# In the second attention, VectorE's product of the query with its rotation table is moved in front of the probabilities' share

## The chip, the cores and the metric

The kernel runs on one core of a Trainium2 chip. The metric is the device time of one execution in microseconds, the median of the runs shown. Five engines work side by side, each through its own in-order list of instructions: TensorE (PE in the profile; its weight loads PEld), VectorE (DVE), ScalarE (ACT), GpSimd (POOL) and SyncE (SP, here the issuer of transfers). They order each other by semaphores: an instruction waits until a counter has reached a value, and those behind it on the same engine wait with it.

## What is computed

Two transformer blocks over 16 batches of 128 rows of 256 values, float32. Each block is an attention against a second input and then a feed-forward part with ternary weights. The change lies in the second attention:

```python
q = rms_norm(x_norm @ Wq.T)                 # 16 heads of 128, batch of 128 rows
k = rms_norm(concat(ctx, x_norm) @ Wk.T)    # 4 key heads, 256 keys
v = concat(ctx, x_norm) @ Wv.T
q, k = rope(q), rope(k)                     # x * cos + rotate_half(x) * sin
probs = softmax(q @ k.T / sqrt(128))        # 4 query heads share a key head
x = x + (probs @ v) @ Wo.T
```

## The kernel before, in words

Five stages follow one another: preparation of the weights, first attention, first feed-forward part, second attention (`part_c`), second feed-forward part. The last four are written as generators that an outer loop advances by one step each, so that neighbouring stages overlap by some steps. In a step, every engine but TensorE takes the earlier stage's instructions first.

`part_c` works on 64 units: 16 batches by 4 groups, a group being one key head with its four query heads. It is a software pipeline with an order written out by hand: in step s each phase treats the unit s minus its lag. The lags are PROJ 4, QK_TURN 5, SCORE 6, PROBS 7, LOWS 8, ATTEND 9, OUT 10. Units 0 to 63 therefore pass PROJ in steps 4 to 67 and PROBS in steps 7 to 70; steps 7 to 67 have both. Every value that goes to TensorE is split into two float16 halves, high and low, and each product is made of three passes.

What a unit needs, with the lines of the profile:

- PROJ: TensorE makes q (six matmuls of 512 columns, L1406), then, once VectorE has let the bank of k and v go (`v_lo`), k and v (L1417). VectorE multiplies q by the table of cosines and sines (`q_cs`, L1330). ScalarE takes the sums of squares of q (L1266, waits for `q_cs`) and k (L1272), evicts v's high half (L1276) and takes the logarithm (L1280) and the reciprocal root `r` (L1301). VectorE scales and rotates k (`k_cs`, L1366, waits for `r`) and makes v's low half (`v_lo`, L1370). GpSimd adds the rotated halves of q (L1189) and splits them (L1193, L1220), and does the same for k (L1223, L1226, L1228); L1202 makes the tables of a later batch.
- SCORE: TensorE makes the scores (L1431); VectorE takes the row maximum (L1351) and turns it into `bias` (L1355); ScalarE takes four exponentials with their row sums in `total` (L1235), the first of them in front of `r`.
- PROBS, one step later: VectorE makes the share, `part` = `total` / 1024 (L1321) and then `share` = 1 / `part` (L1324); ScalarE makes the high halves of the probabilities (`p_hi`, L1252, waits for `share`) in four instructions; VectorE makes the low halves in two pairs, `lows(u, 0)` and `lows(u, 1)` (L1311).
- ATTEND and OUT: TensorE multiplies probabilities by values (L1444) and the result by Wo (L1459); ScalarE and VectorE split the result in between (`a_hi` L1245, `a_lo` L1338).

SP turns the halves by transposing transfers (L1138, L1153, L1159).

In a step of `part_c` VectorE's order is: `part`, `share`, `q_cs`, `a_lo`, `lows` 0, (once per batch the residual, L1345), maximum, `bias`, `lows` 1, `k_cs`, `v_lo`, and then, in one step of four each, the statistics of a new batch (L1376, L1380) or the normalized rows (L1385). The steps with statistics are s = 0, 4, 8, ..., those with rows s = 1, 5, 9, ... ScalarE's order is: `a_hi`, four `p_hi`, the squares of q and k, v's high half, logarithm, (in the steps with rows L1286 and L1289), first exponential, `r`, three exponentials.

Of the kernel before, what the change touches and what calls it, by code (L numbers as in the profile page):

```python
# [21 lines left out]
ALU = mybir.AluOpType  # L22
# [15 lines left out]
def wait(eng, sem, value):  # L38

    if value > 0:  # L40
        eng.wait_ge(sem, value)
# [1012 lines left out]
def part_c(core):  # L1054
# [14 lines left out]
    P_SCALE = 1024.0  # L1069
# [25 lines left out]
    total = c.local("total_c", [P, 2, SHARE])  # L1095
    part = c.local("part_c", [P, 2, SHARE])
    share = c.local("share_c", [P, 2, SHARE])
# [18 lines left out]
    S = {n: c.sem("c_" + n) for n in (  # L1116
        "eps", "stats", "rstd", "y", "y_hi", "y_lo", "tables", "q", "kv", "ss_k", "ss_q", "r", "q_cs", "q_rot", "k_cs",
        "k_rot", "v_hi", "v_lo", "q_hi", "q_lo", "k_hi", "k_lo", "scores", "top", "bias", "exps", "share", "p_hi",
        "p_lo", "attn", "a_hi", "a_lo", "o", "out")}
# [5 lines left out]
    def unit(s, lag):  # L1125

        u = s - lag
        return u if 0 <= u < TOTAL else None

    def batch(s, lag):  # L1130


        u = s - lag
        return u // GROUPS if 0 <= u < TOTAL and u % GROUPS == 0 else None
# [172 lines left out]
    def vector(eng):  # L1307
        def lows(u, half):
            eng.wait_ge(S["p_hi"], 2 * u + half + 1)
            for h in range(2 * half, 2 * half + 2):  # L1310
                last = eng.scalar_tensor_tensor(p_hl[:, u % 2, 1, h, :], s_banks(u)[:, h, :],  # L1311
                                                share[:, u % 2, h:h + 1], p_hl[:, u % 2, 0, h, :],
                                                ALU.mult, ALU.subtract)
            last.then_inc(S["p_lo"], 1)

        for s in range(STEPS + 1):
            probs, proj, score, attend = unit(s, PROBS), unit(s, PROJ), unit(s, SCORE), unit(s, OUT)
            if probs is not None:
                u = probs
                eng.wait_ge(S["exps"], u + 1)  # L1320
                eng.tensor_scalar(part[:, u % 2, :], total[:, u % 2, :], 1.0 / P_SCALE, None, ALU.mult)\  # L1321
                   .then_inc(S["share"], 1)
                eng.wait_ge(S["share"], 2 * u + 1)
                eng.reciprocal(share[:, u % 2, :], part[:, u % 2, :]).then_inc(S["share"], 1)  # L1324
            if proj is not None:
                u, b = proj, proj // GROUPS
                eng.wait_ge(S["tables"], b + 1)
                eng.wait_ge(S["q"], u + 1)
                wait(eng, S["q_rot"], u)
                eng.tensor_tensor(  # L1330
                    q_cs[:, :, :, :],
                    Q_BANK.rearrange("p (h d) -> p h d", h=SHARE).unsqueeze(1).broadcast_to([P, 2, SHARE, HEAD_DIM]),
                    turn["q"][:, b % 2, :, :].unsqueeze(2).broadcast_to([P, 2, SHARE, HEAD_DIM]), ALU.mult)\
                   .then_inc(S["q_cs"], 1)
            if attend is not None:
                u = attend
                eng.wait_ge(S["a_hi"], u + 1)
                eng.scalar_tensor_tensor(a_t[:, u % 2, 1, :], A_BANK, A_SCALE, a_t[:, u % 2, 0, :], ALU.mult,  # L1338
                                         ALU.subtract).then_inc(S["a_lo"], 1)
            if probs is not None:  # L1340
                lows(probs, 0)
            b = batch(s, LAST)
            if b is not None:
                eng.wait_ge(S["o"], GROUPS * (b + 1))
                eng.scalar_tensor_tensor(c.x_rows[:, b, :], O_BANK, 1.0 / (W_SCALE * W_SCALE * P_SCALE * A_SCALE),  # L1345
                                         c.x_rows[:, b, :], ALU.mult, ALU.add).then_inc(S["out"], 1)
            if score is not None:
                u = score
                eng.wait_ge(S["scores"], u + 1)
                wait(eng, S["bias"], u - 1)  # L1350
                eng.tensor_reduce(top[:, u % 2, :], s_banks(u), AX.X, ALU.max).then_inc(S["top"], 1)  # L1351
                eng.wait_ge(S["top"], u + 1)
                eng.wait_ge(S["r"], 2 * (u + 1))
                wait(eng, S["exps"], u - 1)
                eng.scalar_tensor_tensor(bias[:, u % 2, :], top[:, u % 2, :], -1.0, r_q(u), ALU.mult, ALU.mult)\  # L1355
                   .then_inc(S["bias"], 1)
            if probs is not None:
                lows(probs, 1)
            if proj is not None:

                u, b = proj, proj // GROUPS
                eng.wait_ge(S["r"], 2 * (u + 1))
                eng.wait_ge(S["v_hi"], u + 1)
                wait(eng, S["k_rot"], u)
                for n in range(2):
                    last = eng.scalar_tensor_tensor(  # L1366
                        k_cs[:, :, n, :], kv_view[:, n, 0, :].unsqueeze(1).broadcast_to([P, 2, HEAD_DIM]), r_k(u, n),
                        turn["k"][:, b % 2, :, n, :], ALU.mult, ALU.mult)
                last.then_inc(S["k_cs"], 1)
                eng.tensor_tensor(v[:, u % V_SLOTS, 1, :, :], kv_view[:, :, 1, :], v[:, u % V_SLOTS, 0, :, :], ALU.subtract)\  # L1370
                   .then_inc(S["v_lo"], 1)
            b = batch(s, 0)
            if b is not None:
                eng.wait_ge(ffn["out"], b + 1)
                wait(eng, S["stats"], 2 * b)
                eng.bn_stats(stats[:, :], c.x_rows[:, b, :]).then_inc(S["stats"], 1)  # L1376
                eng.wait_ge(S["stats"], 2 * b + 1)
                wait(eng, S["y"], b)
                wait(eng, S["rstd"], 2 * b)
                eng.bn_aggr(mv[:, :], stats[:, :]).then_inc(S["stats"], 1)  # L1380
            b = batch(s, ROWS)
            if b is not None:
                eng.wait_ge(S["rstd"], 2 * (b + 1))
                wait(eng, S["y_lo"], b)
                eng.tensor_scalar(y[:, :], c.x_rows[:, b, :], mv[:, 0:1], rstd[:, :], ALU.subtract, ALU.mult)\  # L1385
                   .then_inc(S["y"], 1)
            yield
# [4 lines left out]
    def tensor(eng):  # L1392
        for s in range(STEPS):
# [69 lines left out]
            yield  # L1463

    return sync, pool, scalar, vector, tensor


# [87 lines left out]
```

## Time and profile before

| | us |
|---|---|
| median of the runs | 799.06 |
| lowest | 797.79 |
| the profiled execution, its own time | 800.01 |
| its span, first to last instruction | 798.3 |
| from the first exponential of step 6 to that of step 66 of `part_c` | 410.28 |

The profiled execution lies 0.1% above the median, and 1.7 us of it lie outside the span. Of the span, 410 us are 60 steps of the second attention. In the rows below, a line of a timeline holds start, duration, engine, line of the kernel, operation, output and inputs, and in brackets the idle time of the engine in front of the instruction with what ended it. Neighbouring instructions of an engine can overlap by some hundredths of a microsecond, so distances are taken from start to start.

### The profile page before, as it was taken

How to read it: one execution, taken by the hardware profiler on the slowest of the kernel's cores; microseconds unless marked ns; L12 is line 12 of the kernel's file. 1: busy time of each engine (PE TensorE's matmuls, PEld its weight loads, DVE VectorE, ACT ScalarE, POOL GpSimd, SP SyncE). 2: the span in 40 equal slices, each digit the busy share in tenths (PEclk: the TensorE clock that was granted, in tenths of full speed). 3: DMA queues.
4: the chain of work that ended last, by engine and by line, in shares of the span. 5: the costliest groups of instructions: out<-in, count | busy, mean ns of one | idle time of the engine just before them, and what ended most of it. 6: DMA issues, size and time to landing. Idle time of an engine off the chain costs nothing. (4 is left out here: it accounts for less than half of the span.)

```text
span 798.3 us, 17290 instructions
## 1 busy us (share of the span) xinstructions
PE 677.3 (85%) x5139; PEld 423.0 (53%) x5139; DVE 661.1 (83%) x1576; ACT 624.3 (78%) x2122; POOL 534.5 (67%) x764
## 2 busy tenths in 40 slices
PE   0075799999578678999999999999999999978995
PEld 0043255455234345666666666666666666645552
DVE  6756556764689769999999999999999999978994
ACT  0556477777399769999999999999999999968661
POOL 1413756663357888888788878887887888753673
PEclk9997599999799989999999999999999999999997
DMA  8502555542024356897887798788879787865244
GB/s 278 199 1 54 138 155 148 142 129 86 11 67 106 64 106 126 147 144 129 148 139 142 127 154 139 134 138 154 139 135 144 143 136 133 153 113 93 58 125 122
DMA packets 323795, 99.80 MB, mean 125 GB/s; under 512 B 294868, under 2 KB 322934, under 8 KB 323446
## 3 DMA queue, kind: packets, MB, share of 16 engines
q1 hardware_dynamic: 323702, 98.70, 61.7%
q8 instruction: 41, 0.67, 0.4%
q14 instruction: 52, 0.43, 0.2%
HBM read 20.01 MB, written 6.29 MB: 33 GB/s over the span
## 5 line engine op out<-in xcount | busy, mean ns | idle before, releaser
L1235 ACT ACTIVATE psum<-psum,arena 128x256 f32<-128x256 f32 x256 | 135.9, 531 | 21.1 <-DVE arena L1355 21.0
L1311 DVE SCALAR_TENSOR_TENSOR arena<-psum,arena 128x256 f16<-128x256 f32 x256 | 110.9, 474 | 1.1 <-ACT arena L1252 1.1
L1252 ACT ACTIVATE arena<-psum,arena 128x256 f16<-128x256 f32 x256 | 100.3, 474 | 7.4 <-issue 3.4
L1444 PE MATMUL psum<-arena 128*128 128x512 f16 x384 | 94.2, 381 | 8.1 <-DVE arena L1338 7.9
L1189 POOL TENSOR_TENSOR arena<-arena 128x512 f32<-128x512 f32 x64 | 81.1, 1267 | 27.8 <-DVE arena L1330 27.8
L1406 PE MATMUL psum<-wq_t,arena 128*128 128x512 f16 x384 | 94.5, 383 | 5.5 <-ACT arena L1266 2.8
L1431 PE MATMUL psum<-arena 128*128 128x256 f16 x768 | 95.6, 275 | 1.0 <-DMA arena<-arena 0.8
L1459 PE MATMUL psum<-wo_t,arena 128*128 128x256 f16 x768 | 95.0, 274 | 0.1
L305 ACT ACTIVATE arena<-psum 128x1024 f32<-128x1024 f32 x64 | 63.1, 1019 | 33.2 <-PE psum L391 33.2
L1459 PEld LDWEIGHTS psum<-wo_t,arena 128*128 128x128 f16 x768 | 75.5, 98 | 23.2 <-issue 1.1
L1220 POOL TENSOR_TENSOR arena<-arena 128x512 f16<-128x512 f32 x64 | 74.1, 1157 | 20.0 <-DVE arena L1355 19.9
L1431 PEld LDWEIGHTS psum<-arena 128*128 128x128 f16 x768 | 75.3, 99 | 11.4 <-DMA arena<-arena 1.6
L1351 DVE TENSOR_REDUCE arena<-psum 128x4 f32<-128x1024 f32 x64 | 77.8, 1215 | 2.7 <-PE psum L1431 2.4
L1330 DVE TENSOR_TENSOR arena<-psum,arena 128x1024 f32<-128x1024 f32 x64 | 78.4, 1225 | 1.1 <-PE psum L1406 1.1
L1266 ACT ACTIVATE arena<-psum 128x128 f32<-128x128 f32 x256 | 68.2, 304 | 10.6 <-DVE arena L1330 10.6
L1417 PE MATMUL psum<-wkv_t,ctx_t 128*128 128x256 f16 x384 | 54.3, 279 | 13.2 <-DVE arena L1370 12.6
L1366 DVE SCALAR_TENSOR_TENSOR arena<-psum,arena 128x256 f32<-128x256 f32 x128 | 56.1, 480 | 9.3 <-ACT arena L1301 6.7
L1223 POOL TENSOR_TENSOR arena<-arena 128x256 f32<-128x256 f32 x64 | 46.3, 724 | 23.7 <-DVE arena L1366 23.6
L422 PE MATMUL psum<-arena 128*32 128x256 f32 x1024 | 61.9, 383 | 0.0
L1266 ACT ACTIVATION_READ_ACCUMULATOR arena<-psum 128x1 f32 x256 | 60.8, 238 | 0.0
L1444 PEld LDWEIGHTS psum<-arena 128*128 128x128 f16 x384 | 33.7, 97 | 48.0 <-issue 13.6
L1417 PEld LDWEIGHTS psum<-wkv_t,ctx_t 128*128 128x128 f16 x384 | 33.2, 99 | 46.9 <-DVE arena L1370 42.3
(187 smaller groups left out, 1612.5 us busy)
## 6 DMA issues: line engine op xcount, KB each, us to landing
arena<-split_scratch SPq DMA_DIRECT2D x96, 64.0 KB, 2.6
arena<-arena SPq DMA_TRANSPOSE x272, 3.3
split_scratch<-arena SPq DMA_DIRECT2D x32, 128.0 KB, 2.1
arena<-in_L_ffn_w SPq DMA_DIRECT2D x2, 1024.0 KB, 6.8
x_rows<-in_L_xattn_Wq SPq DMA_DIRECT2D x1, 2048.0 KB, 14.4
ctx_t<-in_L_xattn_Wo SPq DMA_DIRECT2D x1, 2048.0 KB, 12.4
x_rows<-in_x SPq DMA_DIRECT2D x16, 128.0 KB, 2.3
arena<-in_ctx SPq DMA_DIRECT2D x16, 128.0 KB, 2.5
```

Of the source, the lines that this page charges most:

```text
L1189: eng.tensor_tensor(straight(q_rot[:, :, :]), straight(q_cs[:, 0, :, :]), swapped(q_cs[:, 1, :, :]), ALU.add).then_inc(S["q_rot"], 1)
L1235: last = eng.activation(s_banks(u)[:, h, :], s_banks(u)[:, h, :], ACT.Exp, bias=bias[:, u % 2, h:h + 1], scale=r_q(u)[:, h:h + 1], accum_o ...
L1252: hi = eng.activation(p_hl[:, u % 2, 0, h, :], s_banks(u)[:, h, :], ACT.Copy, scale=share[:, u % 2, h:h + 1])
L1266: last = eng.activation(junk[:, h, :], Q_BANK[:, P * h:P * h + P], ACT.Square, accum_out=sums[:, u % 2, h:h + 1])
L1311: last = eng.scalar_tensor_tensor(p_hl[:, u % 2, 1, h, :], s_banks(u)[:, h, :], share[:, u % 2, h:h + 1], p_hl[:, u % 2, 0, h, :], ALU.mul ...
L1330: eng.tensor_tensor(q_cs[:, :, :, :], Q_BANK.rearrange("p (h d) -> p h d", h=SHARE).unsqueeze(1).broadcast_to([P, 2, SHARE, HEAD_DIM]), tu ...
L1351: eng.tensor_reduce(top[:, u % 2, :], s_banks(u), AX.X, ALU.max).then_inc(S["top"], 1)
L1406: mm = eng.matmul(Q_BANK, y_t[:, b % 2, x, k, :], c.wq_t[:, w, k, SHARE * P * g:SHARE * P * g + SHARE * P], start=(n == 0), stop=(n == 5))
L1417: mm = eng.matmul(KV_BANK[:, KEYS * row:KEYS * row + KEYS], x_t, c.wkv_t[:, w, k, g, :, :].rearrange("p a d -> p (a d)"), start=(n == 0), ...
L1431: mm = eng.matmul(s_banks(u)[:, h, :], q_head(u, q, h), k_keys(u, k), start=(n == 0), stop=(n == 2))
L1444: mm = eng.matmul(A_BANK, v[:, u % V_SLOTS, x, k, :], p_t[:, u % 2, w, :, k, :], start=(n == 0), stop=(n == 5))
L1459: mm = eng.matmul(O_BANK, a_t[:, u % 2, a, P * h:P * h + P], c.wo_t[:, w, SHARE * g + h, :], start=(g == 0 and h == 0 and n == 0), stop=(g ...
```

## The change

Two blocks of VectorE's list change places. In each step with both, `q_cs` now stands in front of `part` and `share`; everything else, on this engine and on the others, keeps its place and its waits.

```diff
         for s in range(STEPS + 1):
             probs, proj, score, attend = unit(s, PROBS), unit(s, PROJ), unit(s, SCORE), unit(s, OUT)
-            if probs is not None:
-                u = probs
-                eng.wait_ge(S["exps"], u + 1)
-                eng.tensor_scalar(part[:, u % 2, :], total[:, u % 2, :], 1.0 / P_SCALE, None, ALU.mult)\
-                   .then_inc(S["share"], 1)
-                eng.wait_ge(S["share"], 2 * u + 1)
-                eng.reciprocal(share[:, u % 2, :], part[:, u % 2, :]).then_inc(S["share"], 1)
             if proj is not None:
                 u, b = proj, proj // GROUPS
                 eng.wait_ge(S["tables"], b + 1)
@@ -1332,6 +1325,13 @@
                    .then_inc(S["q_cs"], 1)
+            if probs is not None:
+                u = probs
+                eng.wait_ge(S["exps"], u + 1)
+                eng.tensor_scalar(part[:, u % 2, :], total[:, u % 2, :], 1.0 / P_SCALE, None, ALU.mult)\
+                   .then_inc(S["share"], 1)
+                eng.wait_ge(S["share"], 2 * u + 1)
+                eng.reciprocal(share[:, u % 2, :], part[:, u % 2, :]).then_inc(S["share"], 1)
             if attend is not None:
```

## Rows read from the trace of the kernel before

**Rows 1.** Stretch: length, busy PE, PEld, DVE, ACT, POOL; PE clock, DMA share, GB/s.
```profile
300.00:696.00 396.00, 386.96 (x2762) 261.45 (x2759) 375.66 (x808) 376.39 (x1649) 321.40 (x419) 1.00 0.81 140
```

**Rows 2.** Waits from 300 to 700 us: total, times, longest.
```profile
ACT psum L1235 <- DVE arena L1355: 15.2, 42, 0.6
DVE arena L1321 <- ACT psum L1235: 12.9, 30, 0.4
```

**Rows 3.** Timeline of VectorE, from one `part` to the next.
```profile
518.94 0.17 DVE L1321 TENSOR_SCALAR arena<-arena 128x4 f32<-128x4 f32 x1 [0.43 <-ACT psum L1235]
519.26 1.23 DVE L1330 TENSOR_TENSOR arena<-psum,arena 128x1024 f32<-128x1024 f32 x1
520.40 0.68 DVE L1338 SCALAR_TENSOR_TENSOR arena<-psum,arena 128x512 f16<-128x512 f32 x1
...
524.01 0.88 DVE L1366 SCALAR_TENSOR_TENSOR arena<-psum,arena 128x256 f32<-128x256 f32 x2
...
525.13 0.42 DVE L1376 BATCH_NORM_STATS2 arena<-x_rows 128x6 f32<-128x256 f32 x1
...
525.68 0.14 DVE L1321 TENSOR_SCALAR arena<-arena 128x4 f32<-128x4 f32 x1
```

**Rows 4.** Timeline of ScalarE in the same step.
```profile
523.23 0.54 ACT L1235 ACTIVATE psum<-psum,arena 128x256 f32<-128x256 f32 x1 [0.24 <-DVE arena L1355]
...
523.78 0.19 ACT L1301 ACTIVATE arena<-arena 128x6 f32<-128x6 f32 x1
```

**Rows 5.** Timeline of TensorE in the same step.
```profile
523.83 1.46 PE L1406 MATMUL psum<-wq_t,arena 128*128 128x512 f16 x6
```

**Rows 6.** Timeline of VectorE and ScalarE in a step where the bias is early.
```profile
300.03 0.17 DVE L1321 TENSOR_SCALAR arena<-arena 128x4 f32<-128x4 f32 x1
...
300.51 1.57 ACT L1252 ACTIVATE arena<-psum,arena 128x256 f16<-128x256 f32 x4 [0.51 <-DVE arena L1324]
...
303.94 0.56 ACT L1235 ACTIVATE psum<-psum,arena 128x256 f32<-128x256 f32 x1
```

**Rows 7.** Timeline of VectorE and ScalarE: high halves to the next bias.
```profile
715.15 1.57 ACT L1252 ACTIVATE arena<-psum,arena 128x256 f16<-128x256 f32 x4 [0.35 <-issue]
...
718.06 0.16 DVE L1355 SCALAR_TENSOR_TENSOR arena<-arena 128x4 f32<-128x4 f32 x1
```

**Rows 8.** Timeline of ScalarE and VectorE in a step with rows.
```profile
498.77 1.57 ACT L1252 ACTIVATE arena<-psum,arena 128x256 f16<-128x256 f32 x4
...
502.66 0.52 ACT L1235 ACTIVATE psum<-psum,arena 128x256 f32<-128x256 f32 x1
...
504.55 0.71 DVE L1385 TENSOR_SCALAR arena<-x_rows,arena 128x256 f32<-128x256 f32 x1
505.18 0.16 DVE L1321 TENSOR_SCALAR arena<-arena 128x4 f32<-128x4 f32 x1
```

**Rows 9.** Timeline of GpSimd: the key's low half in the step of Rows 3.
```profile
526.23 0.67 POOL L1228 TENSOR_TENSOR arena<-arena 128x256 f16<-128x256 f32 x1
```

**Rows 10.** Timeline of all engines where GpSimd runs beside `part`.
```profile
320.07 0.72 POOL L1223 TENSOR_TENSOR arena<-arena 128x256 f32<-128x256 f32 x1
...
320.39 0.44 DVE L1321 TENSOR_SCALAR arena<-arena 128x4 f32<-128x4 f32 x1 [0.43 <-ACT psum L1235]
...
321.12 0.84 ACT L1252 ACTIVATE arena<-psum,arena 128x256 f16<-128x256 f32 x2 [0.28 <-issue]
```

**Rows 11.** Timelines of VectorE and GpSimd where both start together.
```profile
264.38 0.74 DVE L778 TENSOR_TENSOR arena<-arena 128x1 f32<-128x1 f32 x1
...
264.38 0.73 POOL L1202 TENSOR_TENSOR arena<-trig,norm 128x256 f32<-128x256 f32 x1
```

**Rows 12.** Timeline of ScalarE: first exponentials of steps 6 and 66.
```profile
290.89 0.54 ACT L1235 ACTIVATE psum<-psum,arena 128x256 f32<-128x256 f32 x1 [1.63 <-DVE arena L1355]
...
701.17 0.54 ACT L1235 ACTIVATE psum<-psum,arena 128x256 f32<-128x256 f32 x1 [0.58 <-DVE arena L1355]
```

**Rows 13.** Timeline of TensorE after a long gap at the attention's end.
```profile
715.79 2.51 PE L1444 MATMUL psum<-arena 128*128 128x512 f16 x6 [3.47 <-DVE arena L1338]
```

## The prediction, made before the changed kernel ran

> **What bounds the kernel now.** I read the page first (which engines are busy, and when), then busy time by stretch, then the waits, and last the timelines of single steps. From 300 to 696 us TensorE is busy for 386.96 of 396 us, ScalarE for 376.39 and VectorE for 375.66, all at full clock [rows 1]. The three are nearly level, so busy time doesn't decide; the waits do. Two of them face each other: ScalarE's first exponential waits for VectorE's `bias` (42 times, 15.2 us), and VectorE's `part` waits for ScalarE's last exponential (30 times, 12.9 us) [rows 2]. So a step is a loop through two engines: exponentials, `part` and `share`, `q_cs`, `a_lo`, low halves, maximum, `bias`, exponentials. The four exponentials cover `lows` 1, `k_cs` and `v_lo` on VectorE. From first exponential to first exponential the 60 steps 6 to 66 take 701.17 - 290.89 = 410.28 us [rows 12], 6.84 each.
>
> ScalarE has little to spare in it: its idle time before the first exponential is 0.24 us in a plain step [rows 4]. That is the margin by which `p_hi` could come later without cost.
>
> **The change, part by part.** No instruction is added or removed, no transfer moves, and nothing is moved past SP's or GpSimd's lists. There are 61 steps (7 to 67) with both blocks. I count from X, the start of the first exponential.
>
> *q_cs comes earlier.* `k_cs` starts at X+0.78 (523.23 to 524.01), right behind `r`, which ends at X+0.74 [rows 3, 4]. That place is fixed by ScalarE, because `r` stands behind the first exponential. What follows `v_lo` starts 1.12 later, at X+1.90 (525.13) [rows 3]. So `q_cs` starts at X+1.90 if q is there. TensorE's q ends at 523.83 + 1.46 = X+2.06 now [rows 5]; its list starts from the previous step's `v_lo`, so it comes earlier against X by whatever the step grows (now 6.71): X+1.82 at a step of 6.95, X+1.35 at 7.43. No wait for q, barely so at the former. GpSimd's q work behind `q_cs` starts behind the key's, as below; no one waits for it within the step.
>
> *part and share come later.* `q_cs` holds VectorE for 1.14 us, start to next start (519.26 to 520.40) [rows 3]. `part` can start at X+1.90+1.14 = X+3.04. Before, it started as soon as the exponentials were done, after 0.43 us of idling [rows 3]; these end near X+2.4, so they no longer gate it. From `part` to `p_hi` takes 0.48 us (300.03 to 300.51) [rows 6]. `p_hi` would start at X+3.52.
>
> *The cost of being beside GpSimd.* At X+3.04 GpSimd is in the key's low half, L1228. It starts 2.22 us after `k_cs` (524.01 to 526.23) [rows 3, 9], so at X+3.00, and ends at X+3.67. No row shows `part` beside L1228. The nearest rows: beside L1223, also a GpSimd TENSOR_TENSOR, `part` started at 320.39 and took 0.44 us instead of 0.17, until 0.04 after GpSimd's end at 320.79; `p_hi` started 0.33 after that end [rows 10]. A VectorE instruction that started in the same hundredth as a GpSimd TENSOR_TENSOR took 0.74 us for one element per partition, as long as GpSimd's 0.73 [rows 11]. The bounds are thus 0 (no hold, `p_hi` at X+3.52) and the full hold (X+3.67+0.33 = X+4.00), which is 0.48 more. I take the full hold, since GpSimd is ahead by 0.04 us and lost no such tie. The margin is thin, and the lower bound stays in the range.
>
> The Trainium skill, SBUF — State Buffer, section "Who interferes with whom", says that VectorE's `tensor_scalar` can enter a mode that needs the port pair shared with GpSimd, and that whoever issues first keeps it for the whole instruction while the other is blocked. By this rule the plain step has the hold; the 0.44 us of [rows 10] agree with it. Without such a rule one would cost `part` at its usual 0.17 and get the smaller loss below.
>
> *The step that follows.* From `p_hi` to the next first exponential ScalarE needs 3.43 us if nothing holds it (300.51 to 303.94) [rows 6]. The bias is ready sooner: it starts 2.91 after `p_hi` (715.15 to 718.06) [rows 7], ends 0.16 later, and even with the residual's 0.33 in front comes about level with ScalarE. So ScalarE's own list closes the loop, and the stall that VectorE had before `part` turns up before `k_cs`, as a wait for `r`. A plain step takes 4.00 + 3.43 = 7.43 us with the hold, 3.52 + 3.43 = 6.95 without.
>
> *The two batch steps.* Statistics put `part` 0.55 later (525.13 to 525.68) [rows 3]: X+3.59, with 0.08 of GpSimd left, no hold; `p_hi` at X+4.07. The step behind it has the rows' two small activations in ScalarE's list, so its first exponential starts 3.89 behind `p_hi` (498.77 to 502.66) [rows 8] instead of 3.43: 0.46 more. This interval is 4.07+3.43+0.46 = 7.96. Rows put `part` 0.63 later (504.55 to 505.18) [rows 8]: X+3.67, no hold, `p_hi` at X+4.15, interval 7.58.
>
> *The sum.* Of the 60 intervals, 14 follow a statistics step (8 to 60), 14 a rows step, 32 are plain: 32 x 7.43 + 14 x 7.96 + 14 x 7.58 = 237.8 + 111.4 + 106.1 = 455.3 us. Less 410.3 that is +45.0. The 61st reorder, in step 67, adds about 0.7 as a plain one. The feed-forward part behind starts from the attention's end, so nothing later hides it. 800.0 + 45.7 = 845.7 on the profiled execution, which is 0.9 above the median of the runs; I predict 845.
>
> **The rivals.**
> 1. *Forecast, +46 us, chance 0.63*: later share, and GpSimd holds `part`.
> 2. *Later share, no hold*: plain steps of 6.95, 32 x 0.48 = 15.4 less, +30 us, 829 on the median. For it: only one row of before has `part` held for long, and the lead is 0.04. Against: [rows 10, 11]. Chance 0.22.
> 3. *Not slower (the other side)*: `q_cs` fills VectorE's idle time in front of `part` and gives its 12.9 us back: 786. The mechanism is that the loop closes through VectorE's `bias`, not through `p_hi`. It decides where `p_hi` is later by no more than ScalarE's idle time before the exponential, 0.24 us [rows 4]. For it: VectorE's list does lose 0.43 us of waiting in a plain step [rows 3]. Against: `p_hi` is later by 1.14 less the 0.43 gained, at least 0.6 us. Chance 0.06 with its weaker form, in which the two cancel.
> 4. *TensorE loses its clock*: its step of some 6.6 us then has gaps of about 0.8. After a gap of 3.47 us six matmuls of 512 columns took 2.51 us instead of 1.46 [rows 13, 5]; the granted clock had fallen to the lower level, 1.2 of 2.4 GHz. If one step in ten were struck, at 5.7 us more for each (6.6 doubled, less the slack of 0.9), +34 us on top: 879. Against: no gap here nears 3.47. Chance 0.04. The Trainium skill, TensorE: Matmul & The Clock Gate, section "What's actually happening", ties the clock to recent activity; the row agrees, and the rule alone would not strike gaps this short.
> 5. *Every hand-over dearer than the rows*: by 0.15 us a step, 9 us more, 854. Chance 0.05.
>
> **How the numbers follow.** The likeliest case gives 845. Rival 2 sets the lower end: 829 less the error of its sum (0.06 us a step, 4 us) is 825; rival 5 with the same error sets the upper, 858. Outside lie rivals 3 and 4 and a part of the rest. The forecast's own range is 839 to 851. Faster by over 2% (about what a measurement of this kernel can tell from no change): 0.03, half of rival 3; within 2%: 0.04; slower by over 2%: 0.93.
>
> **What would show it.** In the changed profile: `part` at X+3.04 with about 0.66 us, beside L1228, and in the steps behind statistics or rows with 0.17; a plain step of 7.43; almost no wait of ScalarE for `bias` and of VectorE for the exponentials, instead a wait of VectorE for `r` of some 0.3 to 0.8 us a step, and one of ScalarE's `p_hi` for `share`. `part` at 0.17 throughout makes it rival 2. Exponentials that still wait for `bias` in every step would break the forecast: ScalarE would not be what closes the loop. A q that ends after X+1.90 would add a wait before `q_cs` that I cost at nothing.

## The result: 43.8 us slower

| | before | after |
|---|---|---|
| median of the runs, us | 798.67 | 842.48 |
| lowest, us | 797.79 | 841.14 |
| span of the profiled execution, us | 798.3 | 840.9 |
| first exponential of step 6 to that of step 66, us | 410.28 | 453.93 |

The ratio is 1.055, with a 95% interval of 1.053 to 1.0574: 5.5% slower. One of the four executions before took 1745.51 us and is in the median of the table but not in the ratio; without it the median before is 798.29 and the loss 44.2 us. Predicted were 845 and a range of 825 to 858. In the profiled executions the 60 steps of the second attention grew by 43.65 us and the span by 42.6, so the rest of the kernel is unchanged within about 1 us.

Lines behind the moved block have other numbers now: `q_cs` is L1323, `part` L1331, `share` L1334. Busy time by engine in the stretch that answers to [rows 1] (length, then busy PE, PEld, DVE, ACT, POOL, with clock, DMA share and GB/s):

```profile
300.00:734.00 434.00, 384.80 (x2735) 259.07 (x2733) 382.75 (x801) 368.89 (x1629) 319.79 (x415) 1.00 0.73 127
```

TensorE is now busy for 385 of 434 us, at full clock: 49 us of idling where there were 9. No engine has more to do, except VectorE, chiefly in one group (line, engine, operation, output and input, count; busy, mean ns; idle before):

```profile
L1331 DVE TENSOR_SCALAR arena<-arena 128x4 f32<-128x4 f32 x58 | 20.3, 350 | 0.0
```

`part`, four numbers per partition, takes 350 ns on average; before, it took 0.14 to 0.17 us in nearly every step. The waits of the same kernel, from 300 to 735 us (total, times, longest), answer to [rows 2]:

```profile
ACT arena L1252 <- issue: 63.8, 57, 2.0
PE psum L1417 <- DVE arena L1370: 45.7, 57, 1.8
DVE arena L1311 <- ACT arena L1252: 23.2, 58, 1.0
DVE arena L1366 <- ACT arena L1301: 23.1, 43, 0.8
```

Both rows of [rows 2] are gone: ScalarE no longer waits for `bias`, nor VectorE's `part` for the exponentials. In their place ScalarE stands still in front of `p_hi` (the profile names no releaser, "issue"; in the timeline it starts 0.08 us behind the end of `share` each time), and VectorE waits for `r` in front of `k_cs` and for `p_hi` in front of the low halves. TensorE waits for `v_lo`. One plain step in the timelines of VectorE, ScalarE and GpSimd, with X = 508.24:

```profile
507.75 0.16 DVE L1355 SCALAR_TENSOR_TENSOR arena<-arena 128x4 f32<-128x4 f32 x1
508.24 0.60 ACT L1235 ACTIVATE psum<-psum,arena 128x256 f32<-128x256 f32 x1
508.79 0.27 ACT L1301 ACTIVATE arena<-arena 128x6 f32<-128x6 f32 x1
509.09 0.88 DVE L1366 SCALAR_TENSOR_TENSOR arena<-psum,arena 128x256 f32<-128x256 f32 x2 [0.39 <-ACT arena L1301]
510.21 1.22 DVE L1323 TENSOR_TENSOR arena<-psum,arena 128x1024 f32<-128x1024 f32 x1
511.31 0.67 POOL L1228 TENSOR_TENSOR arena<-arena 128x256 f16<-128x256 f32 x1
511.35 0.67 DVE L1331 TENSOR_SCALAR arena<-arena 128x4 f32<-128x4 f32 x1
512.05 0.18 DVE L1334 RECIPROCAL arena<-arena 128x4 f32<-128x4 f32 x1
512.31 1.57 ACT L1252 ACTIVATE arena<-psum,arena 128x256 f16<-128x256 f32 x4 [1.12 <-issue]
...
515.72 0.60 ACT L1235 ACTIVATE psum<-psum,arena 128x256 f32<-128x256 f32 x1
```

The step takes 515.72 - 508.24 = 7.48 us. The first exponential starts 0.49 us after `bias`, so `bias` was ready: ScalarE's own list holds it. `part` starts 0.04 us behind GpSimd's L1228 and ends 0.04 behind it. It can also go the other way, as four steps earlier:

```profile
481.32 0.72 POOL L1228 TENSOR_TENSOR arena<-arena 128x256 f16<-128x256 f32 x1
481.35 0.16 DVE L1331 TENSOR_SCALAR arena<-arena 128x4 f32<-128x4 f32 x1
```

Here GpSimd leads by 0.03 us, and yet VectorE goes through in 0.16 while GpSimd takes 0.05 us longer than usual. Of the 32 steps that the prediction called plain, `part` took 0.59 to 0.67 us in 23; seven went as here, each with GpSimd's L1228 at 0.71 or 0.72 us; and in the first two, where the feed-forward part before still runs, `part` came 0.6 us ahead of L1228 or 0.42 behind it (0.16 and 0.28 us). Behind statistics and rows `part` took 0.15 or 0.16 throughout. In the steps behind rows it is not ScalarE's own list that closes the step: there `bias` ends 0.04 us before the next first exponential.

### The profile page after: what moved, and what is told of

The parts are those of the page before. It is cut to its first block and busy times, and to the rows that moved or that the text cites. A ratio compares the mean times of both kernels' runs of the same rounds, so it can differ in the third digit from the quotient of the medians.

```text
span 840.9 us, 17290 instructions
## 1 busy us (share of the span) xinstructions
PE 675.6 (80%) x5139; PEld 421.2 (50%) x5139; DVE 672.7 (80%) x1576; ACT 620.3 (74%) x2122; POOL 535.1 (64%) x764
## 5 line engine op out<-in xcount | busy, mean ns | idle before, releaser
L1235 ACT ACTIVATE psum<-psum,arena 128x256 f32<-128x256 f32 x256 | 141.4, 568 | 3.1 <-DVE arena L1355 3.1
L1431 PEld LDWEIGHTS psum<-arena 128*128 128x128 f16 x768 | 75.1, 98 | 9.5 <-issue 0.9
L1323 DVE TENSOR_TENSOR arena<-psum,arena 128x1024 f32<-128x1024 f32 x64 | 77.8, 1215 | 0.7 <-PE psum L1406 0.7
L1235 ACT ACTIVATION_READ_ACCUMULATOR psum<-psum,arena 128x1 f32 x256 | 60.2, 235 | 0.0
```

The costliest lines, as they stand in the source:

```text
L1235: last = eng.activation(s_banks(u)[:, h, :], s_banks(u)[:, h, :], ACT.Exp, bias=bias[:, u % 2, h:h + 1], scale=r_q(u)[:, h:h + 1], accum_o ...
L1323: eng.tensor_tensor(q_cs[:, :, :, :], Q_BANK.rearrange("p (h d) -> p h d", h=SHARE).unsqueeze(1).broadcast_to([P, 2, SHARE, HEAD_DIM]), tu ...
L1431: mm = eng.matmul(s_banks(u)[:, h, :], q_head(u, q, h), k_keys(u, k), start=(n == 0), stop=(n == 2))
```

## The experiments

All were timed beside the kernel before: its median was 799.78 us for after_pool_late, after_no_part, after_r_first and before_no_part, 798.25 for split_no_part and after_no_part_r_first, and 798.64 for the others. "The old order" is the kernel before, "the new order" the changed kernel.

| run | us | ratio to before, 95% interval | steps 6 to 66, us |
|---|---|---|---|
| after_pool_late | 833.44 | 1.042 (1.0402 to 1.0437) | 442.86 |
| after_no_part | 825.01 | 1.0312 (1.0292 to 1.0332) | 434.89 |
| after_r_first | 821.45 | 1.0277 (1.0255 to 1.0298) | 432.33 |
| after_no_part_r_first | 807.20 | 1.0107 (1.009 to 1.0124) | 418.57 |
| before_no_part | 791.77 | 0.9897 (0.9881 to 0.9914) | 402.48 |
| before_r_first | 796.47 | 0.9972 (0.9959 to 0.9984) | 408.14 |
| before_no_part_r_first | 785.70 | 0.9839 (0.9819 to 0.986) | 398.19 |
| before_alo_first | 851.85 | 1.067 (1.0649 to 1.0691) | 461.44 |
| before_q_split | 822.16 | 1.0296 (1.0275 to 1.0317) | 432.11 |
| split_no_part | 799.11 | 1.0006 (0.9993 to 1.0018) | 409.41 |

The theory that the runs test has three parts. The share's delay goes straight into the step, through ScalarE's list. GpSimd's L1228 holds `part`. And `r`, behind the first exponential, fixes where VectorE's later blocks stand.

### Is it GpSimd that holds `part`? after_pool_late

```diff
                 eng.wait_ge(S["k_hi"], u + 1)
+                for n in range(3):
+                    eng.memset(idle[:, n:n + 1], 0.0)
                 eng.tensor_tensor(k_hl(u, 1), flat(k_rot[:, :, :]), k_hl(u, 0), ALU.subtract).then_inc(S["k_lo"], 1)
```

`idle` is a new scratch tile of three columns; its allocation isn't shown.

> The changed kernel with three one-column GpSimd memsets on a scratch tile between the wait and the key's low half, so that this instruction starts a few hundredths of a us later than VectorE's part instead of before it; nothing else moves. If part is held by GpSimd's TENSOR_TENSOR (theory): part falls from 0.67 to about 0.16 us in the 23 steps where it was held, each step gets 0.5 us shorter, 11.5 us in all, near 831 us, although instructions were added. If the 0.67 us has another cause (a semaphore, VectorE's own pipeline): part stays long, 842 us.

Measured: 833.44. Timelines of GpSimd and VectorE in this run, a plain step:

```profile
509.18 0.16 POOL L1230 MEMSET idle_c<- 128x1 f32 x3
509.23 0.16 DVE L1334 TENSOR_SCALAR arena<-arena 128x4 f32<-128x4 f32 x1
509.29 0.67 POOL L1231 TENSOR_TENSOR arena<-arena 128x256 f16<-128x256 f32 x1
```

Three more instructions on GpSimd push its key instruction 0.06 us behind `part` (here L1334), and `part` takes 0.15 to 0.18 us in every step but one of the beginning, where GpSimd's instruction had started 0.33 us ahead of it (0.36 us). The 60 steps take 11.07 us less; the ratios differ by 1.3%, some 10 us. That settles the hold and its price. What is left in this run, 34 us over before, is not this hold's.

### Without `part`: after_no_part and before_no_part

```diff
-                eng.tensor_scalar(part[:, u % 2, :], total[:, u % 2, :], 1.0 / P_SCALE, None, ALU.mult)\
-                   .then_inc(S["share"], 1)
-                eng.wait_ge(S["share"], 2 * u + 1)
-                eng.reciprocal(share[:, u % 2, :], part[:, u % 2, :]).then_inc(S["share"], 1)
+                eng.reciprocal(share[:, u % 2, :], total[:, u % 2, :]).then_inc(S["share"], 2)
```

with `P_SCALE` = 1 instead of 1024 and `A_SCALE` = 1 instead of 1/1024.

> The changed kernel with the scale of 1/1024 on the probabilities left out (and the matching 1/1024 behind the attention): VectorE takes one reciprocal straight from the row sums, and part is gone. Theory: the held instruction is gone and no other takes its place, since a reciprocal beside the same GpSimd instruction took its usual 0.18 us before; 11.5 us for the hold and 0.2 us in each of 61 steps for part itself, 24 in all, near 819 us. If the hold goes over to the reciprocal: only the 12 us of part itself, 830 us. If the share is not on the path: 842 us.

> The kernel before with part left out in the same way. Theory: the loop exponentials, share, VectorE's list, bias is what sets its step of 6.71 us, so 0.2 us less of it shortens the step until TensorE's own list (about 6.6 us) takes over: 0.1 us a step, 7 us in all, near 792 us. Rival, TensorE sets the step already: 799 us.

Measured: 825.01 and 791.77. The old order came out as expected: the share is on the path there too, for about 8 us of the 12 that `part` costs. The new order came out 6 us above the expectation, though the reciprocal was held nowhere (0.16 or 0.17 us, also when it started 0.03 us behind L1228). In the 60 steps 19.0 us were gained (453.93 to 434.89) where 23.7 were expected. Two things took the rest. The first is q; ScalarE, TensorE and VectorE in one plain step:

```profile
502.65 0.60 ACT L1235 ACTIVATE psum<-psum,arena 128x256 f32<-128x256 f32 x1
503.24 1.46 PE L1403 MATMUL psum<-wq_t,arena 128*128 128x512 f16 x6
504.29 0.41 DVE L1367 TENSOR_TENSOR arena<-psum,arena 128x256 f16<-128x256 f32 x1
504.79 1.23 DVE L1323 TENSOR_TENSOR arena<-psum,arena 128x1024 f32<-128x1024 f32 x1
```

`q_cs` follows `v_lo` at a distance of 0.50 us instead of 0.33: q ends at 504.70, and `q_cs` starts at X+2.14. With shorter steps TensorE's q is late for its new place in front of the share, by 0.17 us in this step and by up to that in 14 of the 60. Before the change the same q ended at X+2.06 and no one minded [rows 5].

The second is another hold, in the steps behind rows. They still take 7.58 us, though `p_hi` comes 0.20 earlier. GpSimd, VectorE (`bias`) and ScalarE (first exponential):

```profile
495.23 0.67 POOL L1215 TENSOR_TENSOR arena<-arena 128x256 f16<-128x256 f32 x1
495.51 0.41 DVE L1352 SCALAR_TENSOR_TENSOR arena<-arena 128x4 f32<-128x4 f32 x1
495.95 0.54 ACT L1235 ACTIVATE psum<-psum,arena 128x256 f32<-128x256 f32 x1
```

`bias` takes 0.41 us instead of 0.16, until 0.02 behind the end of GpSimd's L1215 (the low half of a new batch's rows), and the exponential follows 0.03 later. So it went in 13 steps here; in the changed kernel `bias` came later beside L1215 and took 0.20 in the same 13 steps.

### Where does VectorE's place come from? after_r_first and before_r_first

```diff
+            u = unit(s, PROJ)
+            if u is not None:
+                ...
+                eng.activation(r[:, u % 8, :], log_ms[:, :], ACT.Exp, scale=-0.5).then_inc(S["r"], 1)
             score = unit(s, SCORE)
             if score is not None:
                 ...
                 exponential(score, 0)
-            u = unit(s, PROJ)
-            if u is not None:
-                ...
-                eng.activation(r[:, u % 8, :], log_ms[:, :], ACT.Exp, scale=-0.5).then_inc(S["r"], 1)
```

> The changed kernel with one move in ScalarE's list: the reciprocal root r in front of the first exponential instead of behind it. Theory: k_cs waits for r, and k_cs sets where v_lo, q_cs and so part start; with r early k_cs starts about 0.37 us sooner after p_hi and each step gets shorter by that, up to 22 us in all; GpSimd's key instructions move with k_cs, so the holds stay or grow by some steps: 820 to 828 us. If VectorE's place in the loop does not hang on r: 842 us.

> The kernel before with r in front of the first exponential. Theory: there k_cs doesn't close the loop, so the early r gives nothing on VectorE; it only takes r's 0.1 us out from between the exponentials into ScalarE's idle time before them, so they end 0.1 us sooner: 0.09 us a step, near 794 us, against 21 us in the changed kernel. If k_cs sets the step before as well: 785 us or less. If the exponentials' end doesn't matter: 799 us.

Measured: 821.45 in the new order, 21 us less, and 796.47 in the old, 2 us less where 5 were expected. So `r` is on the new order's loop and hardly on the old one's. Timeline of the new order with `r` first, VectorE and ScalarE:

```profile
506.32 0.16 DVE L1355 SCALAR_TENSOR_TENSOR arena<-arena 128x4 f32<-128x4 f32 x1
507.26 0.88 DVE L1366 SCALAR_TENSOR_TENSOR arena<-psum,arena 128x256 f32<-128x256 f32 x2
507.02 0.21 ACT L1296 ACTIVATE arena<-arena 128x6 f32<-128x6 f32 x1
507.14 0.52 ACT L1235 ACTIVATE psum<-psum,arena 128x256 f32<-128x256 f32 x1
```

`k_cs` starts 0.12 us after the first exponential, not 0.85. GpSimd still holds `part` in 24 steps, since the key instructions move along with `k_cs`. In the old order the early `r` brought the end of the exponentials forward by 0.1 us, but put `part` (at X+2.31 behind rows) 0.07 us behind the start of GpSimd's L1226, the key's high half. GpSimd and VectorE:

```profile
421.70 0.40 POOL L1226 CAST arena<-arena 128x256 f16<-128x256 f32 x1
421.78 0.34 DVE L1321 TENSOR_SCALAR arena<-arena 128x4 f32<-128x4 f32 x1
```

`part` took 0.34 to 0.36 us in these steps, one of four, which ate the gain there: they take 7.13 us, against 7.14 before.

### Another block in front of the share: before_alo_first

```diff
+            if attend is not None:
+                u = attend
+                eng.wait_ge(S["a_hi"], u + 1)
+                eng.scalar_tensor_tensor(a_t[:, u % 2, 1, :], A_BANK, A_SCALE, a_t[:, u % 2, 0, :], ALU.mult,
+                                         ALU.subtract).then_inc(S["a_lo"], 1)
             if probs is not None:
                 u = probs
                 eng.wait_ge(S["exps"], u + 1)
```

and the same block taken out of its old place behind `q_cs`.

> The kernel before with another block, a_lo, in front of the share instead of q_cs. a_lo waits for a_hi, which ends 2.88 us after the first exponential starts, so part comes at 3.52 instead of 2.42 and p_hi at about 4.0. Theory, what matters is when the share is ready: a plain step of 7.43 us as in the changed kernel, near 840 us. Rival, what costs is q_cs itself beside the exponentials and GpSimd's key work: q_cs is in its old place here, so 799 to 810 us.

Measured: 851.85, even worse than the change. The rival, that `q_cs` beside the exponentials costs by itself, falls: `q_cs` is in its old place here and the loss is larger. My number was 12 us low. Half of the plain steps take 7.47 us, about the 7.43 expected, but the others 7.8 to 8.0, and in 14 steps `part` took 0.55 us:

```profile
507.31 0.67 POOL L1228 TENSOR_TENSOR arena<-arena 128x256 f16<-128x256 f32 x1
507.45 0.55 DVE L1326 TENSOR_SCALAR arena<-arena 128x4 f32<-128x4 f32 x1
```

I had placed GpSimd where it stood in the old order. With `q_cs` later, GpSimd's list was later too in the steps with most work (L1228 at X+3.38 instead of X+3.0), and `part` started 0.14 us behind its start. Behind rows it was `bias` that took 0.45 us, until the end of GpSimd's L1202; these steps take 7.82 us.

### Half the dose: before_q_split and split_no_part

```diff
+            if proj is not None:
+                u, b = proj, proj // GROUPS
+                ...
+                eng.tensor_tensor(q_cs[:, 0:1, :, :], ..., turn["q"][:, b % 2, 0:1, :]..., ALU.mult)
             if probs is not None:
                 ...
             if proj is not None:
                 u, b = proj, proj // GROUPS
-                eng.tensor_tensor(q_cs[:, :, :, :], ...
+                eng.tensor_tensor(q_cs[:, 1:2, :, :], ..., turn["q"][:, b % 2, 1:2, :]..., ALU.mult)
```

> The change at half the dose: q_cs in two instructions of half the size, the cosine half in front of part and share, the sine half behind them. Theory: the half comes into VectorE's 0.43 us of idle time, share is later by 0.2 us, inside the margin of 0.24 us before the first exponential, so the loss of 44 us is gone; but q_cs now stands behind TensorE's q and in front of share, a loop of two steps of about 6.7 us, so nothing is won either: 797 to 803 us. If any delay of share costs its full size: 812 us. If filling the idle time pays by itself: 790 us or less.

> The half dose (q_cs split around the share) without part, its power of two taken out on both sides. In the half dose part came at 3.12 to 3.14 us after the first exponential in the steps behind statistics and rows, just behind GpSimd's key instruction at 3.09, and took 0.62 and 0.56 instead of 0.16 us. If that hold is what the half dose cost (31 held steps, about 0.5 us each, and 0.2 us for part in each of 61): 822 less 15 and less some 8 to 12, 795 to 800 us. If the cost is q_cs in front of the share by itself: 812 us or more.

Measured: 822.16, far above my 797 to 803, and 799.11 once `part` was out, inside 795 to 800. The first expectation failed because it looked at plain steps alone. In the steps behind statistics and rows `part` came 0.5 us later, right behind GpSimd:

```profile
510.02 0.67 POOL L1228 TENSOR_TENSOR arena<-arena 128x256 f16<-128x256 f32 x1
510.10 0.62 DVE L1330 TENSOR_SCALAR arena<-arena 128x4 f32<-128x4 f32 x1
```

These two of four steps take 7.95 and 7.57 us; in split_no_part they take 7.29 and 6.95. The plain pair takes 6.36 and 6.94 with `part`, 6.65 on average against 6.71 before: in the second, `q_cs` waits for q as above. So half the block in the idle time wins 0.06 us in a plain step and still loses in the batch steps; split_no_part is 7 us slower than the old order without `part` (791.77).

### What is left of the order: before_no_part_r_first and after_no_part_r_first

Both edits together, in either order.

> The kernel before with both part left out (its power of two taken out on both sides of the attention) and r in front of the first exponential. Theory: the two gains lie on one loop and add up until TensorE's list of about 6.55 us closes the step; 0.2 and 0.1 us of loop are taken away, some 0.15 us a step come out: 787 to 790 us. If TensorE already sets the step without part: 792 us.

> The changed order with the three costs that the theory names taken away: no part (so no hold) and r in front of the first exponential. Theory: what closes the loop then is q: TensorE's list from v_lo to the end of q (6.7 us), q_cs, share, p_hi, bias, k_cs, v_lo, 13.3 us over two steps, 6.65 a plain step, with the batch steps near 7.1: 798 to 808 us, still 12 to 22 above the old order with the same two edits (785.7). If the gains add up as measured one by one from 842.5 (17.5 and 21): 804 us. If another cost of the order is left: 815 us or more.

Measured: 785.70, a little under the 787 to 790 expected, and 807.20, inside 798 to 808. The old order with both edits is the fastest kernel of this study, 1.6% under the kernel before. In the new order 21.5 us of the loss remain when neither the hold nor `r` is in the way. VectorE then waits for q in front of `q_cs` in 14 steps (waits from 300 to 690 us):

```profile
ACT arena L1252 <- issue: 23.3, 52, 1.3
DVE arena L1323 <- issue: 6.5, 14, 0.5
```

From these pairs the loss of 43.8 us divides like this: some 10 us are the hold (842.48 to 833.44, or 11.07 us in the 60 steps). Without `part` the two orders are 825.01 - 791.77 = 33.2 apart, with `r` first besides 807.20 - 785.70 = 21.5. So 12 us come from `r` standing behind the exponential, and 21.5 from the share behind a longer block, the batch steps' work in front of it, the late q, and `bias` held behind rows (0.41 us in 13 steps of after_no_part_r_first too). These last four were not measured one by one. The split is that of the kernels without `part`: with it the same move of `r` is worth 21.0 us in the new order and 2.2 in the old.

## Why the prediction was right, point by point

- **The bound.** The two waits that faced each other before were taken for the two ends of a loop, with ScalarE 0.24 us short of closing it itself. Both waits vanished together, and ScalarE closed it, but for the steps behind rows, where `bias` was later by 0.07 us; the prediction had the two about level there.
- **q_cs.** It was to start at X+1.90, without a wait for q. It starts at X+1.97 in the step shown (510.21 - 508.24) and finds q ready. The warning that the margin is thin in shorter steps was right: in after_no_part it was gone.
- **The hold.** Predicted 0.66 us and full in all 32 plain steps; measured 0.59 to 0.67 in 23. The step of the prediction that failed, if slightly, is "lost no such tie": at a lead of 0.02 to 0.03 us GpSimd lost seven times. The trace of before had shown that it can. In its 14 steps behind rows GpSimd's L1226 starts less than 0.01 us ahead of `part`, and `part` goes through in 0.15 or 0.16 us while L1226 takes 0.42 instead of 0.40:

```profile
340.95 0.42 POOL L1226 CAST arena<-arena 128x256 f16<-128x256 f32 x1
340.95 0.16 DVE L1321 TENSOR_SCALAR arena<-arena 128x4 f32<-128x4 f32 x1
```

The shared-port rule that stood behind the prediction, of the Trainium skill, SBUF — State Buffer, "Who interferes with whom", agrees with the runs in that `part`, where it waits, waits to the end of GpSimd's instruction. The rule goes by who issues first; at a lead of some 0.03 us and less in the profile's start times both results occur here, so these times don't tell it. Where `part` was 0.05 us or more ahead (after_pool_late), it was never held.
- **The step.** Plain with the hold 7.43, measured 7.41 to 7.50 in all but two (7.57 and 7.69); without it 6.95, measured 6.89 to 6.97; behind statistics 7.96, measured 8.03 (8.39 in the first); behind rows 7.58, measured 7.58 or 7.59.
- **The sum.** 455.3 us for the 60 steps, measured 453.93. The seven steps in which VectorE won are 3.4 us less than costed; the steps behind statistics are 1.4 us more, the other plain ones 0.5. The first two steps had no full hold and yet took 7.39 and 7.45 us, because `q_cs` came at X+2.3 there, beside the feed-forward part. The errors partly cancel, so 845 against 842.5 is in part luck.
- **The rivals.** The smaller loss without a hold (829) is nearly what after_pool_late measured when the hold was taken away (833). A gain from filling the idle time was seen in no whole kernel; at half the dose it was 0.06 us in a plain step, and the batch steps lost more. TensorE kept full clock from 300 to 734 us, with its idle time five times as long.

## What to carry to other kernels

Idle time in front of an instruction is no room for a block if what stands behind that instruction feeds another engine: ask who waits for the result, and how much that engine has to spare (here 0.24 us against a block of 1.14). If the answer is a loop through two engines, also ask what then fixes the block's own start; here it was a small activation behind the first exponential, worth 21 us in one order and 2 in the other. Small VectorE instructions between two SBUF tiles on such a loop (here `part` and `bias`) deserve a look at what GpSimd runs at that very time, and another look after each change, since a shorter step moved the hold from one to the other: taking a scale by a power of two out of the loop removed one of them and gave 1% in the old order.

## What the hardware did that I had not expected

- Whether VectorE's small TENSOR_SCALAR or GpSimd's TENSOR_TENSOR goes first was open at a lead of 0.02 to 0.04 us for GpSimd: VectorE waited 22 times and won seven (one more wait had a lead of 0.10). When it won, GpSimd's instruction took 0.71 or 0.72 instead of 0.67 us. In before_q_split, at a lead of 0.01 to 0.02 us, VectorE won ten times and waited twice. A CAST on GpSimd held `part` too when it was 0.07 us ahead (0.34 to 0.36 us in before_r_first). A RECIPROCAL of the same shape took its 0.16 or 0.17 us in after_no_part, where it started 0.03 us behind the same GpSimd instruction.
- Three added GpSimd instructions made the kernel 9 us faster.
- When ScalarE runs without a gap, its results come some hundredths later: an exponential took 0.60 us instead of 0.54, and `r` 0.27 instead of 0.19, though the distances from start to start stayed at 0.54 to 0.65. `k_cs` therefore started at X+0.85 in the steps with statistics and in the second plain step of each pair, not at the X+0.78 of [rows 3]; that is the 0.07 by which their intervals are longer. In the plain steps right behind a step with rows, where ScalarE had waited for `bias`, it was X+0.79.
